# Two feed-forward stacks: a new order of all engines, with the halves of scores and of weighing mostly side by side

## The chip, the cores and the metric
The kernel runs on one core of a Trainium2 chip. The metric is the device time of the whole program in microseconds. Before the change it is 3801.89 us, the median of three runs (3801.88 to 3802.43).

## The reference
The input is a batch of 4 sequences of 512 tokens with 128 features. The residual stream goes through four parts, each on the layer-normed stream: a retention attention, a stack of six layers, an RWKV-like mixer, and the same stack again with the same weights.

```python
x = x + attn_a(layernorm(x)); x = x + stack(layernorm(x))
x = x + attn_b(layernorm(x)); x = x + stack(layernorm(x))

# stack: DEPTH = 6 layers, 16 heads of 64, windows of 32 tokens
for i in range(DEPTH):
    x = attn_layer(shift_tokens(x), Wqkv[i], q_scale[i], k_scale[i], Wo[i]) + x
    x = ffn_layer(shift_tokens(x), ln_g[i], ln_b[i], W1[i], b1[i], W2[i], b2[i]) + x

# attn_layer: q and k are l2-normed per head and rotated; each window of 32 queries
# sees its own and the previous window of keys, masked; softmax; times values; @ Wo
# ffn_layer: layernorm, (xn @ W1 + b1) split in a and gate, a * gelu(gate) @ W2 + b2
```

Everything is float32. The change is in the stack, which runs twice and takes most of the time.

## The kernel before
A stack is cut into 96 **tiles** of 128 tokens (6 layers x 4 sequences x 4 tiles). Four tiles of one sequence in one layer are a **group**; a stack has 24. The group g of a layer needs the residual stream that group g - 4 of the layer before has left. The residual stream of all sequences lies transposed in `xst`, features on partitions.

What a tile goes through, with the engine in brackets: `stage` copies its 128 columns of `xst` to `xs` (GpSimd, L1230); `project` makes six products of 512 columns, k0, q0, k1, q1, v0 and v1, each in one bank of PSUM (TensorE, L584); `rotate` reads a q or k bank twice and multiplies with cosines and sines (VectorE, L1038), `rope` adds these (GpSimd, L1238), `square` reads the same bank (ScalarE, L876), `sum_squares` and `norms` make the inverse lengths (VectorE) with `guess` (ScalarE) between, and `unit` multiplies them in (GpSimd, L1247). `turn` transposes a chunk with four matmuls (L595), `keep` copies it out (ScalarE, L897). `scores` is in two halves of 64 small matmuls on 64x32 parts of the array (L604), into two banks of its own. Then `mask_max`, `off_max`, `exponent`, `sum_probs`, `invert`, `scale_probs`, on VectorE, GpSimd and ScalarE. `turn_probs` transposes the probabilities in two halves, `probs_out` copies them out. `weigh` multiplies with values, in two halves of 64 small matmuls on 64x64 parts (L629). The values come by ten DMAs a tile from `v_nat` to `v_w` (`spread_values`, SyncE, L515) after `values_out`. `heads_out` copies weighed heads out, one half at a time (ScalarE, L936), `project_out` multiplies them with Wo (L647), `mid` adds them to the residual stream (VectorE, L1115).

What a group goes through when its four tiles are done: `center`, `center_square`, `center_out`, `variance`, `inv_std`, `mid_norm`, `gain_bias`; six products `up` (gate and lin, 0 to 2), three `gelu` and three `hidden`, one `down` of three accumulated products, and `finish`, which adds to the stream (VectorE, L1144).

All products but scores and weighing share four PSUM banks, `work`. Which item writes which bank is a table, `BANK`, with an entry for each of the four slots. Both halves of weighing write the same 256 columns of `bank_o`, so the second half of a tile has to wait until the first is copied out, and stands in the next slot.

The order is written out by hand for each engine, in a function `slot(N, T, G, at, of)`. A stack is 96 + 12 **slots**; slot N has T = N mod 4. `at(3)` is tile N - 3, `of(2)` is the group two before this slot's. `run_slots` (L482) unrolls 16 slots, then a loop of two rounds with 32 slots, then 28. On TensorE a wait stands ahead of most items: the bank that it writes must have been read. Such a wait reads `wait(pe, "squared_k0", N - 2)`. In the loop, `apart` puts a count-up of a semaphore between waits and matmuls of scores and weighing.

The order of TensorE before, in slot 1, without its waits:

```
q1(3) gate1 v1(5) weigh1(7) T.q0(4) T.k0(4) P1(6) T.q1(4) k0(2) q0(2) scores0(4) P0(6)
out(7) weigh0(6) T.k1(4) k1(2) v0(4) scores1(4) lin2
```

Here `k0` is a projection, `T.k0` a turn, `P0` a turn of probabilities, `out` is `project_out`; the number in brackets is how many slots the tile is behind. The other three slots have the same tile items in nearly the same order; lin 0 and gate 2 are in slot 0, lin 1 in slot 2, `center` in slot 2, `variance`, `down` and gate 0 in slot 3.

## Time and profile before

| | |
|---|---|
| median of 3 runs | 3801.89 us |
| profiled execution, its span | 3803.9 us |
| TensorE busy | 3594.4 us (94%), 61680 matmuls |
| VectorE busy | 3264.6 us (86%) |
| GpSimd busy | 2752.8 us (72%) |
| ScalarE busy | 2374.7 us (62%) |
| `project`, L592 | 1148.0 us busy, 2304 matmuls, 604 ns each |
| `weigh`, L641 | 437.0 us busy, 24576 matmuls, 221 ns each |
| `scores`, L615 | 330.4 us busy, 24576 matmuls, 224 ns each |
| `square`, L883 | 443.3 us busy, 768 instructions, 594 ns each |
| `stage`, L1236 | 4 in a group, 1.2 us busy, 293 ns each |

A matmul on float32 is two instructions in the profile. Matmuls are pipelined: their durations overlap, so the cost of a group of them is seen from start to start, not from a mean. The profiled execution lasts as long as its span; nothing lies around it. The first stack runs from about 106 to 1736 us, the second from 2171 to 3799.

### The profile page before, as it was taken

What the parts mean: (1) busy time and instruction counts of PE and PEld (TensorE: products, weight loads), DVE (VectorE), ACT (ScalarE), POOL (GpSimd) and SP (SyncE); (2) the same over time, 40 slices, a digit from 0 to 9 for tenths busy, and PEclk for the clock granted to TensorE, in tenths of its full rate; (3) what the DMA queues carried; (4) which work ended last, traced back from release to release, by engine and by line L of the source; (5) the groups of instructions that cost most, each with busy time, mean ns of one, the idle gap of its engine ahead of it and who ended that gap; (6) DMA issues with size and microseconds to landing.
All of it is one profiled execution on the core that took longest, in us unless ns stands there. A gap on an engine that the chain in (4) does not pass through costs nothing. (4 is left out here: it accounts for less than half of the span.)

```text
span 3803.9 us, 157044 instructions
## 1 busy us (share of the span) xinstructions
PE 3594.4 (94%) x61680; PEld 2336.5 (61%) x61680; DVE 3264.6 (86%) x11515; ACT 2374.7 (62%) x4331; POOL 2752.8 (72%) x2632
## 2 busy tenths in 40 slices
PE   6799999999999999997699689999999999999998
PEld 4466666666666666662466456666666666666665
DVE  6898888888888889865799798889898888889885
ACT  2567667666766767663422257667676766767665
POOL 1788888878888888852144288888887888888883
PEclk9899999999999999998799699999999999999999
DMA  1232323323322332220000132233233232332222
GB/s 46 77 85 71 81 73 78 87 67 74 85 73 69 85 75 66 66 65 16 0 1 6 29 81 72 74 87 78 71 80 76 71 81 74 83 78 68 66 69 57
DMA packets 170286, 250.95 MB, mean 66 GB/s; under 512 B 36544, under 2 KB 67264, under 8 KB 169408
## 3 DMA queue, kind: packets, MB, share of 16 engines
q1 hardware_dynamic: 169536, 240.72, 25.4%
q8 instruction: 499, 8.18, 0.9%
q14 instruction: 251, 2.06, 0.2%
HBM read 38.21 MB, written 1.05 MB: 10 GB/s over the span
## 5 line engine op out<-in xcount | busy, mean ns | idle before, releaser
L592 PE MATMUL stack_work<-stack_w_qkv,stack_xs 128*128 128x512 f32 x2304 | 1148.0, 604 | 34.4 <-ACT stack_sq L883 17.8
L1244 POOL TENSOR_TENSOR stack_roped<-stack_rot_c,stack_rot_s 128x512 f32<-128x512 f32 x768 | 984.6, 1304 | 148.5 <-DVE stack_rot_s L1052 148.2
L1254 POOL TENSOR_TENSOR stack_roped<-stack_roped,stack_rnorm 128x512 f32<-128x512 f32 x768 | 794.6, 1045 | 188.7 <-DVE stack_rnorm L1084 188.7
L883 ACT ACTIVATE stack_sq<-stack_work 128x512 f32<-128x512 f32 x768 | 443.3, 594 | 485.6 <-DVE stack_rot_s L1052 485.1
L1050 DVE TENSOR_TENSOR stack_rot_c<-stack_work,rot_tables 128x512 f32<-128x512 f32 x768 | 526.8, 686 | 130.4 <-PE stack_work L592 112.9
L592 PEld LDWEIGHTS stack_work<-stack_w_qkv,stack_xs 128*128 128x128 f32 x2304 | 400.5, 191 | 384.4 <-issue 323.9
L1270 POOL TENSOR_TENSOR stack_s_m<-stack_s_m,stack_inv 128x512 f32<-128x512 f32 x384 | 400.8, 1044 | 276.4 <-DVE stack_inv L1113 276.1
L1052 DVE TENSOR_TENSOR stack_rot_s<-stack_work,rot_tables 128x512 f32<-128x512 f32 x768 | 521.6, 679 | 0.0
L1061 DVE TENSOR_REDUCE stack_ssq<-stack_sq 128x8 f32<-128x512 f32 x768 | 496.7, 667 | 6.0 <-issue 4.4
L641 PEld LDWEIGHTS stack_bank_o<-stack_p_t,stack_v_w 64*64 64x64 f32 x24576 | 394.5, 135 | 171.9 <-issue 147.4
L600 PE MATMUL stack_work<-ident,stack_roped 128*128 128x128 f32 x3072 | 452.2, 280 | 8.3 <-issue 5.8
L1095 DVE CUSTOM_DVE_ANT_0 stack_s_m<-stack_bank_s,band 128x64 f32<-128x64 f32 x3072 | 449.4, 217 | 7.4 <-PE stack_bank_s L615 7.4
L615 PEld LDWEIGHTS stack_bank_s<-stack_k_t,stack_q_t 64*32 64x32 f32 x24576 | 268.3, 105 | 289.1 <-issue 287.4
L641 PE MATMUL stack_bank_o<-stack_p_t,stack_v_w 64*64 64x32 f32 x24576 | 437.0, 221 | 1.4 <-issue 1.4
L1262 POOL TENSOR_TENSOR stack_s_m<-stack_s_m,stack_smax 128x512 f32<-128x512 f32 x384 | 401.2, 1045 | 2.9 <-DVE stack_smax L1095 2.7
L600 PEld LDWEIGHTS stack_work<-ident,stack_roped 128*128 128x128 f32 x3072 | 338.2, 141 | 77.7 <-issue 53.3
L655 PE MATMUL stack_work<-stack_o_t,stack_w_o 128*128 128x128 f32 x3072 | 374.6, 275 | 1.7 <-DVE stack_hid L1141 1.7
L655 PEld LDWEIGHTS stack_work<-stack_o_t,stack_w_o 128*128 128x128 f32 x3072 | 358.1, 192 | 3.3 <-DVE stack_hid L1141 3.3
L676 PE MATMUL stack_work<-stack_x_c,stack_w 128*128 128x512 f32 (+1 forms) x576 | 309.7, 621 | 27.4 <-ACT stack_hid L983 21.7
L615 PE MATMUL stack_bank_s<-stack_k_t,stack_q_t 64*32 64x64 f32 x24576 | 330.4, 224 | 0.0
L909 ACT COPY stack_q_t<-stack_work 128x512 f32<-128x512 f32 x384 | 230.5, 600 | 112.2 <-PE stack_work L600 101.3
L933 ACT COPY stack_p_t<-stack_work 128x512 f32<-128x512 f32 x384 | 228.9, 596 | 56.1 <-PE stack_work L626 55.7
(257 smaller groups left out, 5269.0 us busy)
## 6 DMA issues: line engine op xcount, KB each, us to landing
stack_v_w<-stack_v_nat SPq DMA_DIRECT2D x1152, 128.0 KB
stack_v_w<-stack_v_nat SPq DMA_DIRECT2D x768, 64.0 KB
stack_w_qkv<-table_ffn_qkv SPq DMA_DIRECT2D x192, 96.0 KB, 2.3
stack_w_o<-table_ffn_wo SPq DMA_DIRECT2D x12, 512.0 KB, 4.2
stack_w<-table_ffn_w SPq DMA_DIRECT2D x12, 384.0 KB, 3.3
stack_w<-table_ffn_w SPq DMA_DIRECT2D x12, 192.0 KB, 3.1
x_outer<-L_attn_a_X SPq DMA_DIRECT2D x4, 256.0 KB, 6.9
ret_xpos<-table_xpos SPq DMA_DIRECT2D x1, 1024.0 KB, 6.2
```

The lines of the kernel that those rows point to most:

```text
L592: pe.matmul(bank[:, :], xs[:, T, :], w_qkv[:, g.half, col:col + 512], start=True, stop=True).then_inc(done["proj_" + c], 1)
L600: last = pe.transpose(bank[:, P * n:P * (n + 1)], roped[:, CHUNKS.index(c), T % 2, P * n:P * (n + 1)], ident[:, :])
L615: last = pe.matmul(bank_s[j][WINDOW * n:WINDOW * (n + 1), 64 * hp:64 * hp + 64], q_t[rows, T % 2, hp, WINDOW * n:WINDOW * (n + 1)], k_t[ro ...
L641: last = pe.matmul(bank_o[HD * odd:HD * (odd + 1), gp, at:at + WINDOW], v_w[64 * gp:64 * gp + 64, T % 2, n, 2 * m + j, :], p_t[64 * gp:64 ...
L655: last = pe.matmul(bank[:, 0:P], w_o[:, g.half, n, :], o_t[:, T % 2, n, :], start=n == 0, stop=n == PAIRS - 1)
L883: act.activation(sq[:, i % 2, :], work[(BANK["p_" + c][T] + g.row) % 4][:, :], ACT.Square).then_inc(done["squared_" + c], 1)
L1050: dve.tensor_tensor(rot_c[:, i % 2, :].rearrange("p (h d) -> p h d", h=8), src.rearrange("p (h d) -> p h d", h=8), cosine, ALU.mult)
L1052: dve.tensor_tensor(rot_s[:, i % 2, :].rearrange("p (h f d) -> p h f d", h=8, f=2), src.rearrange("p (h f d) -> p h f d", h=8, f=2)[:, :, ...
L1061: dve.tensor_reduce(ssq[:, T % 2, i, :], sq[:, i % 2, :].rearrange("p (h d) -> p h d", h=8), AX.X, ALU.add).then_inc(done["summed_" + c], 1)
L1095: last = dve.tensor_tensor_reduce(s_m[:, T % 2, j, hp, :], bank_s[j][:, 64 * hp:64 * hp + 64], mask[:, first:first + 2 * WINDOW], 1.0, LOW ...
L1244: pool.tensor_tensor(roped[:, i, T % 2, :], rot_c[:, i % 2, :], rot_s[:, i % 2, :], ALU.add).then_inc(done["roped_" + c], 1)
L1254: pool.tensor_tensor(r, r, rnorm[:, T % 2, i, :].unsqueeze(2).broadcast_to([P, 8, HD]), ALU.mult).then_inc(done["united_" + c], 1)
```

## The change
All six bodies and tables of the order are replaced; the helpers change where they must.

```diff
 # TensorE: reads the residual stream itself
-    pe.matmul(bank[:, :], xs[:, T, :], w_qkv[:, g.half, col:col + 512], start=True, stop=True
+    pe.matmul(work[(BANK["p_" + c][T] + g.row) % 4][:, :], xst[:, g.row, P * T:P * (T + 1)],
+              w_qkv[:, g.half, col:col + 512], start=True, stop=True).then_inc(done["proj_" + c], 1)
 # before the first projection of a tile
-    wait(pe, "staged", t)
+    if c == FIRST_IN and T == 0:
+        wait_x(pe, g.number - BATCH)
...
 # weigh: the halves have columns of their own
-    m, at = 2 * half + odd, P * half + WINDOW * n
+    m, at = 2 * half + odd, P * (2 * j + half) + WINDOW * n
...
 # ScalarE: one copy a tile
-            def heads_out(t, T, g, j):
+            def heads_out(t, T, g):
-                wait(act, f"weighed{j}", t)
+                wait(act, "weighed1", t)
                 wait(act, "pe_wo", t - 2)
-                act.copy(o_t[:, T % 2, 4 * j:4 * j + 4, :].rearrange("p (g h) n -> p g h n", g=2),
-                         bank_o[:, :, 0:2 * P].rearrange("p g (h n) -> p g h n", h=2)
-                         ).then_inc(done[f"ot_set{j}"], 1)
+                act.copy(o_t[:, T % 2, :, :].rearrange("p (j g h) n -> p j g h n", j=2, g=2),
+                         bank_o[:, :, :].rearrange("p g (j h n) -> p j g h n", j=2, h=2)).then_inc(done["ot_set"], 1)
...
 # TensorE, slot 0, the beginning
+                    wait_group(pe, "hid0", G - 3)
+                    project(*at(0), "k0")
+                    wait(pe, "v_out0", N - 3)
+                    turn(*at(2), "q0")
+                    wait(pe, "pt_set0", N - 5)
+                    project(*at(3), "v1")
+                    wait(pe, "ot_set", N - 6)
+                    weigh(*at(5), 0)
+                    wait(pe, "pt_set1", N - 5)
+                    turn(*at(2), "k0")
+                    wait(pe, "squared_k0", N - 0)
+                    up(of(3), "gate", 1)
...
 # GpSimd
-                stage(*at(0))
```

The new order of TensorE, in the notation above:

```
slot 0: k0(0) T.q0(2) v1(3) weigh0(5) T.k0(2) gate1 q0(0) P0(4) weigh1(5) gate2 T.k1(2) out(6)
        T.q1(2) q1(0) lin2 k1(0) scores0(2) scores1(2) T.k1(1) T.k0(1) v0(2) out(5) P1(4) v1(2) T.q0(1)
slot 1: k0(0) T.q1(2) weigh0(5) weigh1(5) lin1 q0(0) P0(4) center k1(0) scores0(2) scores1(2)
        variance P1(4) down v1(2) q1(0) weigh0(4) weigh1(4) T.k0(1) T.q0(1) T.k1(1)
slot 2: k0(0) v0(3) q0(0) scores0(2) T.q1(2) P1(4) q1(0) scores1(2) P0(4) gate0 k1(0)
        weigh0(4) weigh1(4) T.k0(1) v1(2) v0(2)
slot 3: k0(0) out(7) T.q1(2) q0(0) T.q0(2) k1(0) out(6) T.k1(2) q1(0) scores0(2) scores1(2)
        lin0 v0(2) P0(4) P1(4)
```

The orders of ScalarE, VectorE and GpSimd are now also written out for each slot. ScalarE in slot 0, where two gelus of a group stand:

```
square k0(0), values_out 1(3), guess(1), keep k0(2), gelu 1, probs_out 0(4), square q0(0), heads_out(5), gelu 2,
table load, keep k1(2), keep q1(2), exponent 1(3), square q1(0), square k1(0), exponent 0(3), keep k1(1), ...
```

GpSimd has four `rope` and four `unit` in every slot, and beside them three `off_max` and two `scale_probs` in slot 0, two and three in slot 1 (one of the three for the tile four behind), three and none in slot 2, none and three in slot 3. `log_var` and `inv_std` are one function before and two after. The turns back to natural layout at a stack's end stand together in slot 96 + 9.

## Rows read from the trace of the kernel before
**Rows 1.** The page: the span, and a DMA issue with its microseconds to landing.
```profile
span 3803.9 us, 157044 instructions
...
stack_w_qkv<-table_ffn_qkv SPq DMA_DIRECT2D x192, 96.0 KB, 2.3
```
**Rows 2.** Busy us by stretch: TensorE, weight loads, VectorE, ScalarE, GpSimd; granted clock; DMA.
```profile
105.90:228.00 122.10, 105.42 (x1868) 63.65 (x1868) 112.51 (x395) 66.60 (x132) 101.25 (x99) 0.94 0.27 68
...
824.40:895.30 70.90, 66.99 (x1255) 44.07 (x1256) 57.55 (x222) 45.62 (x84) 53.77 (x52) 0.98 0.28 70
1024.05:1089.85 65.80, 65.34 (x1256) 43.14 (x1255) 58.71 (x222) 45.83 (x84) 53.76 (x53) 1.00 0.30 73
```
**Rows 3.** Timeline of VectorE at two neighbouring `finish`: start, us, instruction, idle before.
```profile
1024.05 1.52 DVE L1153 SCALAR_TENSOR_TENSOR stack_xst<-stack_work,stack_vec,stack_mshift 64x512 f32<-64x512 f32 x2 [2.52 <-PE stack_work L685]
...
1089.85 1.52 DVE L1153 SCALAR_TENSOR_TENSOR stack_xst<-stack_work,stack_vec,stack_mshift 64x512 f32<-64x512 f32 x2 [2.52 <-PE stack_work L685]
```
**Rows 4.** Timeline of TensorE's matmuls, from 1042 to 1056 us.
```profile
1042.15 1.95 PE L655 MATMUL stack_work<-stack_o_t,stack_w_o 128*128 128x128 f32 x16
1044.04 1.14 PE L641 MATMUL stack_bank_o<-stack_p_t,stack_v_w 64*64 64x32 f32 x64
1045.10 0.66 PE L600 MATMUL stack_work<-ident,stack_roped 128*128 128x128 f32 x4
1045.59 1.02 PE L592 MATMUL stack_work<-stack_w_qkv,stack_xs 128*128 128x512 f32 x2
1046.45 1.02 PE L676 MATMUL stack_work<-stack_x_c,stack_w 128*85 128x512 f32 x2
1047.31 1.02 PE L592 MATMUL stack_work<-stack_w_qkv,stack_xs 128*128 128x512 f32 x2
1048.26 0.86 PE L615 MATMUL stack_bank_s<-stack_k_t,stack_q_t 64*32 64x64 f32 x64
1049.05 1.12 PE L676 MATMUL stack_work<-stack_x_c,stack_w 128*128 128x512 f32 x2
1050.01 1.02 PE L592 MATMUL stack_work<-stack_w_qkv,stack_xs 128*128 128x512 f32 x2
1051.49 1.12 PE L676 MATMUL stack_work<-stack_x_c,stack_w 128*128 128x512 f32 x2 [0.46 <-ACT stack_hid L983]
...
1053.41 1.14 PE L641 MATMUL stack_bank_o<-stack_p_t,stack_v_w 64*64 64x32 f32 x64
1054.47 1.09 PE L600 MATMUL stack_work<-ident,stack_roped 128*128 128x128 f32 x8
1055.40 0.60 PE L626 MATMUL stack_work<-ident,stack_s_m 128*128 128x128 f32 x4
```
**Rows 5.** Timeline of the weight loads of one half of scores and one of weighing.
```profile
1048.26 0.70 PEld L615 LDWEIGHTS stack_bank_s<-stack_k_t,stack_q_t 64*32 64x32 f32 x64 [0.76 <-issue]
...
1053.41 1.02 PEld L641 LDWEIGHTS stack_bank_o<-stack_p_t,stack_v_w 64*64 64x64 f32 x64 [0.76 <-issue]
```
**Rows 6.** Timeline of ScalarE at the gelu that TensorE waits for.
```profile
1049.46 1.28 ACT L983 ACT_TABLE_LOAD   x1
1050.76 0.68 ACT L983 ACTIVATE stack_hid<-stack_work,stack_vec 85x512 f32<-85x512 f32 x1
```
**Rows 7.** Instructions by line from 1024.1 to 1089.9: count, busy us, mean ns, idle before.
```profile
L941 ACT COPY stack_o_t<-stack_bank_o 128x512 f32<-128x512 f32 x8 | 4.7, 593 | 0.8 <-PE stack_bank_o L641 0.8
...
L1244 POOL TENSOR_TENSOR stack_roped<-stack_rot_c,stack_rot_s 128x512 f32<-128x512 f32 x16 | 20.6, 1308 | 2.8 <-DVE stack_rot_s L1052 2.8
L1254 POOL TENSOR_TENSOR stack_roped<-stack_roped,stack_rnorm 128x512 f32<-128x512 f32 x17 | 17.6, 1044 | 3.9 <-DVE stack_rnorm L1084 3.9
...
L1270 POOL TENSOR_TENSOR stack_s_m<-stack_s_m,stack_inv 128x512 f32<-128x512 f32 x8 | 8.4, 1044 | 5.3 <-DVE stack_inv L1113 5.3
...
L1050 DVE TENSOR_TENSOR stack_rot_c<-stack_work,rot_tables 128x512 f32<-128x512 f32 x16 | 11.0, 687 | 2.3 <-PE stack_work L592 2.0
```
**Rows 8.** Timeline of SyncE's queue: three of a tile's ten value DMAs.
```profile
1056.16 1.87 SPq L531 DMA_DIRECT2D stack_v_w<-stack_v_nat  x3
```

More of the change, by code:

```diff
@@ L661, in center, with variance @@
                 wait(pe, "mid_set", 4 * g.number + 3)
-                pe.matmul(bank[:, :], center_m[:, :], mshift[:, g.pair, 0:SEQ], start=True, stop=True
+                pe.matmul(work[(BANK["ct"] + g.row) % 4][:, :], center_m[:, :], mshift[:, g.pair, 0:SEQ], start=True, stop=True
                           ).then_inc(done["pe_center"], 1)
-            def variance(g, bank):
+            def variance(g):
                 if not live_group(g):
@@ L668, in variance, with up @@
                 wait_group(pe, "center_sq", g)
-                pe.matmul(bank[:, :], mean_m[:, :], c_sq[:, :], start=True, stop=True).then_inc(done["pe_var"], 1)
-            def up(g, kind, k, bank):
+                pe.matmul(work[(BANK["va"] + g.row) % 4][:, :], mean_m[:, :], c_sq[:, :], start=True, stop=True
+                          ).then_inc(done["pe_var"], 1)
+            def up(g, kind, k):
                 if not live_group(g):
@@ new lines, in slot @@
+                    wait(pe, "kept_q0", N - 2)
+                    project(*at(0), "q0")
+                    wait(pe, "v_out1", N - 3)
+                    turn_probs(*at(4), 0)
+                    weigh(*at(5), 1)
+                    wait(pe, "kept_k0", N - 2)
+                    up(of(3), "gate", 2)
+                    wait_group(pe, "gelu1", G - 3)
+                    turn(*at(2), "k1")
+                    wait(pe, "squared_q0", N - 0)
+                    project_out(*at(6))
+                    wait(pe, "pt_set0", N - 4)
@@ new lines, in slot @@
+                    turn(*at(2), "q1")
+                    wait_group(pe, "gelu2", G - 3)
+                    project(*at(0), "q1")
+                    wait(pe, "kept_k1", N - 2)
+                    up(of(3), "lin", 2)
+                    wait(pe, "mid_set", N - 6)
+                    project(*at(0), "k1")
+                    wait(pe, "masked0", N - 3)
+                    wait(pe, "masked1", N - 3)
+                    scores(*at(2), 0)
+                    scores(*at(2), 1)
+                    wait(pe, "kept_q1", N - 2)
@@ new lines, in slot @@
+                    turn(*at(1), "k1")
+                    wait(pe, "squared_q1", N - 0)
+                    turn(*at(1), "k0")
+                    wait_group(pe, "hid2", G - 3)
+                    project(*at(2), "v0")
+                    wait(pe, "squared_k1", N - 0)
+                    project_out(*at(5))
+                    wait(pe, "kept_k1", N - 1)
+                    turn_probs(*at(4), 1)
+                    wait(pe, "kept_k0", N - 1)
+                    project(*at(2), "v1")
+                    wait(pe, "v_out0", N - 2)
@@ L1229, in _ @@
         def _(pool):
-            def stage(t, T, g):
-                if not live(t):
-                    return
-                wait_x(pool, g.number - BATCH)
-                wait(pool, "proj_" + LAST_IN, t - 4)
-                apart(pool, t)
-                pool.tensor_copy(xs[:, T, :], xst[:, g.row, P * T:P * (T + 1)]).then_inc(done["staged"], 1)
             def rope(t, T, g, c):
```

652 lines of the change are left out of this document (374 added, 278 removed).

## The prediction
> **What bounds the kernel now.** I read the page's busy shares first, then busy time by stretch. In one group of four tiles, 1024.05 to 1089.85, TensorE is busy for 65.34 of 65.80 us, VectorE for 58.71, GpSimd for 53.76, ScalarE for 45.83; the granted clock is 1.00, the 2.4 GHz level [rows 2]. So a stack is set by what TensorE is given to do and in what order, and the other three have 11 to 30% to spare. The group is the beat: `finish` (L1153) comes once a group, at 1024.05 and again at 1089.85 [rows 3]. There are 24 groups in a stack, 48 in all. One group of each stack is longer: 824.4 to 895.3 is 70.9 us with TensorE busy for 66.99; that is the loop's way back, which stays. While a stack fills (105.9 to 228) VectorE is busy for 112.5 of 122.1 us: there VectorE decides more than TensorE [rows 2].
>
> Busy is not the same as useful. In TensorE's timeline the difference of two starts is what an item costs. Two projection matmuls with 512 columns (a **pair**, also `up`, `center`, `variance`; `down` is three) cost 0.86 us (1046.45 to 1047.31). `project_out` costs 1.89 in front of a weighing (1042.15 to 1044.04). Four transposes (a **turn**, `turn_probs` too) take 0.49 behind a weighing (1045.10 to 1045.59) and eight take 0.93 there (1054.47 to 1055.40), so one costs 0.435 and the place behind a weighing about 0.06. A half of scores or of weighing is 64 small matmuls on parts of the array; I call it an **island**. It costs 0.79 for scores (1048.26 to 1049.05) and 1.06 for weighing (1053.41 to 1054.47) [rows 4], more than its matmuls, in three places:
> - in front: the pair before one takes 0.95 instead of 0.86 (1047.31 to 1048.26), +0.09; without it `project_out` is 1.80;
> - at its end: scores are busy for 0.86 with a last matmul of 0.22, so that one starts at 0.64, and the next item 0.15 later; weighing 0.92, then 0.14. Steps inside average 0.64/63 = 0.01 and 0.92/63 = 0.015;
> - behind: 0.06 for a turn, as above, and 0.10 for a pair (1049.05 to 1050.01) [rows 4].
> The weight-load queue shows why: the loads of an island start 0.76 us after the load before them has ended, none under the matmul in front [rows 5].
>
> That adds up. Before, a group is 32 pairs x 0.86 = 27.52, 24 turns x 0.435 = 10.44, 4 `project_out` x 1.80 = 7.20, `down` 2.58: 47.74. Islands 8 x 0.79 + 8 x 1.06 = 14.80, 16 fronts x 0.09 = 1.44, behind them 12 turns x 0.06 + 4 pairs x 0.10 = 1.12. Sum 65.10, against 65.80 measured. The missing 0.70 has its place: the pair at 1050.01 lasts until 1051.49, where `up` gate 1 waits for a gelu; it is the only idle time that TensorE's timeline shows in the group [rows 4]. ScalarE gives that gelu behind a table load of 1.28 [rows 6].
>
> **What the change does to that sum.** The matmuls stay the same in number and shape; the stationary operand is read from the residual stream in place of its copy. What goes are borders. In the new order scores are adjacent in slots 0, 1 and 3 and apart in slot 2; weighing is apart in slot 0, adjacent twice in slot 1 and once in slot 2. So 16 islands become 10: three double and two single ones of each kind. 47.74 stays. Double scores cost 0.64 + 0.01 + 0.79 = 1.44, double weighing 0.92 + 0.015 + 1.06 = 2.00, so the islands are 3 x 1.44 + 3 x 2.00 + 2 x 0.79 + 2 x 1.06 = 14.02; 10 fronts 0.90; behind them stand 6 turns (0.36) and 4 pairs (0.40). Sum **63.42**, 1.68 less.
>
> The unknown in it is the joint. Between two halves stand waits (`kept_k1`, `kept_q1`, or `pt_set1`) and in the loop a count-up. No row shows these in the middle of an island. From below they cost nothing; from above as much as an end, a front and what is behind, 0.15 + 0.09 + 0.06, so that next to nothing of 1.68 is left. Weighing is near the lower end: its 64 weight loads are spread over 1.02 us, so instructions arrive faster than they are used. Scores take theirs in 0.70 [rows 5] and have less cover; I give each of their three joints 0.05. That makes 63.57, 1.53 less.
>
> The Trainium skill says in "TensorEngine Tiling (Array Packing)", Key Properties, that changing the tiling mode drains TensorE, while changing only the tile does not. By that rule the joints are free and the sum is 63.42; the trace agrees as to the borders (0.09 in front, 0.15 at the end), and no run here shows a joint.
>
> **What TensorE waits for in the new order.** Each item writes one of four banks, and the next to write it waits for its reader. I take the TensorE time between the two. A square comes after two VectorE instructions of 0.69 [rows 7] and ends its own 0.59, about 2.1 us in all; a copy of 0.59 ends after about 0.75. The shortest distance to a square is the same before and after: pair 0.95, weighing 1.12, two turns 0.87, = 2.95 (after: from k0 in slot 0 to gate 1). The shortest to a copy is three turns, 1.31, before, and four, 1.73, after. Distances of this size hold today, since the one wait is for a gelu [rows 4]. In slot 0 gate 1 now ends 4.7 us after the slot's start and its gelu is asked for at 8.1; table load and gelu are 1.28 + 0.68 [rows 6], and what ScalarE has before them is done by about 4.4. Gate 2 ends at 8.1 and is asked for at 10.7, behind `heads_out` alone. So the 0.70 may go. Tighter is what follows: the table goes back (1.28), then k1 is copied at about 11.0 and asked for at 11.6. I take 0.3 of waiting a group instead of 0.70, between none and 1.5.
>
> `heads_out` is one copy of 1024 columns instead of two of 512 with 0.59 each [rows 7]: between one and two of these, I take 1.05, on an engine busy for 45.8 of 65.8 us. A weighing may start only behind the copy of the tile before; in slot 1 the two are about 10 us apart, so it is hidden, with 8 us of room. The removed staging is 4 x 0.29 us on GpSimd (table above), where nothing waited for it; TensorE waits for the residual itself, finished some three slots earlier. The value DMAs are ten a tile at 0.62 us of issue [rows 8], and a DMA of that queue lands 2.3 us after its issue [rows 1]: 8.5 us. ScalarE's next value copy waits for them: in slots 1 and 2 they can start at 3.4 and 2.3 us and are asked for at 13.7 and 11.8. Hidden by 1 to 2 us.
>
> VectorE's work per group, 58.7 us, stays: 92% of 63.9. GpSimd's 53.8 less 1.2 is 82%, but unevenly spread: slots 2 and 3 last about 25.1 us on TensorE and give GpSimd 8 ropes x 1.31, 8 units x 1.04 and 6 others x 1.04 = 25.1 [rows 7].
>
> **The sum.** 63.57 + 0.30 = 63.87 a group, 1.93 less than 65.80. It counts in 46 of 48 groups: while a stack fills, VectorE covers one group's worth. 46 x 1.93 = 88.8. Fill and drain I leave as they are (`finish` comes 13 slots after a group's first projection instead of 12), with 8 us each way. The profiled execution is its span, 3803.9 us [rows 1]: 3803.9 - 88.8 = 3715.1. It is 2.0 above the median of the runs, 3801.89, so I forecast **3713 us**.
>
> **Rivals.**
> - **A. The joints cost like borders.** For it: nothing in the trace shows a joint. Against: the loads of an island follow each other without a pause [rows 5]. Then only waiting falls by 0.4: 46 x 0.4 = 18, 3784. Half of it is 46 x 1.24 = 57, 3745.
> - **B. New waits eat a part.** The order of four engines is new, and ScalarE has 0.6 us of room behind the table load. At 1.5 us a group instead of 0.30: 46 x (65.80 - 65.07) = 34, 3768.
> - **C. GpSimd becomes the bound (the other side).** Its place is slots 2 and 3, with 25.1 us of work in 25.1 us. Today it idles for 12.0 of 65.8 us, waiting for VectorE's inverses, norms and rotations (5.3, 3.9 and 2.8) [rows 7]. If it idles there in the same share, 4.6 us, and slots 0 and 1 don't catch up, a group takes 63.57 + 4.6 = 68.2: 46 x 2.4 = 109 more, 3911. From 2.2 us of lost time a group on it is slower than before; at 3 us it is 3837. Against: turns lie one or two slots behind their units, so that slots 0 and 1 can catch up.
> - **D. Fill and drain get longer** by what the groups save: that needs 44 us a stack, a third of the whole fill's 122 us [rows 2]. Nothing speaks for it.
>
> **How the numbers follow.** My case 0.62, with its own range 3690 to 3740. A 0.10, of it 0.03 at no change; B 0.14; C 0.10; D 0.01; better than 3690 (no waiting at all, 48 x 2.38 = 114) 0.03. A measurement of this kernel tells 0.2% (7.6 us) from no change. Faster 0.86, same 0.03, slower 0.11. The range goes down to all of the islands and waits and 8 us of fill (3680), and up to the middle of A and B and some way beyond: 3785.
>
> **What would show it.** Right: two `finish` of neighbouring groups 63.4 to 64.2 us apart; double scores of 1.4 to 1.5 us and double weighing of 2.0 from start to the next item; ten fronts of 0.09; the gelu wait gone or moved; `heads_out` x192 of about 1.05 us. Wrong, by the joint: double scores over 1.6. Wrong, by waits: TensorE rows with idle time behind a square, a copy or a united chunk, and GpSimd busy over 90% in a group.

## The result, and the profile after
The changed kernel takes **3844.76 us** (median of 4 runs, 3843.56 to 3848.38) against 3802.16 (3801.88 to 3806.66) for the kernel before: ratio 1.0107, 95% interval 1.0093 to 1.012. It is 1.1% slower; the forecast was 2.3% faster. The page of the changed kernel:
```profile
span 3843.6 us, 156240 instructions
...
PE 3557.4 (93%) x61680; PEld 2340.8 (61%) x61680; DVE 3250.6 (85%) x11515; ACT 2368.7 (62%) x4135; POOL 2707.1 (70%) x2440
...
L591 PE MATMUL stack_work<-stack_w_qkv,stack_xst 128*128 128x512 f32 x2304 | 1175.4, 607 | 71.4 <-ACT stack_sq L885 43.2
...
L1112 DVE TENSOR_REDUCE stack_ssq<-stack_sq 128x8 f32<-128x512 f32 x768 | 513.9, 669 | 70.1 <-ACT stack_sq L885 69.6
...
L642 PE MATMUL stack_bank_o<-stack_p_t,stack_v_w 64*64 64x32 f32 x24576 | 415.6, 220 | 16.0 <-issue 14.5
...
L615 PE MATMUL stack_bank_s<-stack_k_t,stack_q_t 64*32 64x64 f32 x24576 | 320.8, 225 | 33.9 <-issue 33.9
```
TensorE's busy time fell, as forecast, its idle time rose by more. Idle time grew in two places: behind a square (L885), 43.2 us at the projections against 17.8 before, with 69.6 us of VectorE's that the kernel before does not have; and "issue" in scores and weighing, which was 0.0 and 1.4 us before.

Busy time by stretch (columns as in [rows 2]): the fill of stack 1, the twenty groups behind it, and one group without a stop inside an island, 65.44 us, that answers to the 65.80 of [rows 2]:
```profile
106.70:308.80 202.10, 177.16 (x3269) 112.14 (x3270) 175.70 (x648) 117.05 (x219) 163.27 (x149) 0.94 0.28 70
308.80:1645.00 1336.20, 1294.18 (x25081) 865.26 (x25081) 1166.47 (x4440) 916.14 (x1601) 1055.27 (x960) 1.00 0.30 74
1120.47:1185.91 65.44, 64.24 (x1255) 42.91 (x1254) 58.94 (x223) 44.88 (x80) 51.96 (x48) 1.00 0.31 76
```
Cut at `finish`, stack 1 is: fill (first projection to first `finish`) 202.1 us against 189.1, twenty groups 1336.2 against 1321.5, drain 116.6 against 118.9. Stack 2: 200.0 against 188.8, 1337.7 against 1321.9, 108.5 against 116.1. Groups were 65.8 each; now they run from 65.3 to 70.8 (72.6 and 72.8 at the loop's way back, 70.9 and 71.2 before). The long ones are the first after the fill and after the loop's way back.

TensorE's timeline in the first group of the twenty (columns as in [rows 4]) shows what was right and the first thing that was missed:
```profile
322.37 2.07 PE L642 MATMUL stack_bank_o<-stack_p_t,stack_v_w 64*64 64x32 f32 x128
324.37 0.66 PE L600 MATMUL stack_work<-ident,stack_roped 128*128 128x128 f32 x4
324.86 1.88 PE L591 MATMUL stack_work<-stack_w_qkv,stack_xst 128*128 128x512 f32 x4
327.41 1.12 PE L591 MATMUL stack_work<-stack_w_qkv,stack_xst 128*128 128x512 f32 x2 [0.66 <-ACT stack_sq L885]
...
332.46 1.12 PE L591 MATMUL stack_work<-stack_w_qkv,stack_xst 128*128 128x512 f32 x2 [0.41 <-DVE stack_mshift L1174]
```
Double weighing costs 324.37 - 322.37 = 2.00 us, exactly the sum's number. In double scores the step from the first half's last matmul to the second half's first is 0.017 us (median of 144), less than the longest steps inside every half (0.03 to 0.06): the **joint is free**. By the Trainium skill ("TensorEngine Tiling (Array Packing)", Key Properties) a change of tile alone drains nothing; the runs agree, with 0.017 us across the joint and 2.00 for double weighing.

The whole account of the group without a stop can be read from TensorE's rows:
```profile
1136.38 1.89 PE L591 MATMUL stack_work<-stack_w_qkv,stack_xst 128*128 128x512 f32 x4
1139.05 1.13 PE L591 MATMUL stack_work<-stack_w_qkv,stack_xst 128*128 128x512 f32 x2 [0.78 <-ACT stack_sq L885]
1140.01 1.95 PE L656 MATMUL stack_work<-stack_o_t,stack_w_o 128*128 128x128 f32 x16
...
1143.10 0.60 PE L600 MATMUL stack_work<-ident,stack_roped 128*128 128x128 f32 x4
1144.12 1.12 PE L591 MATMUL stack_work<-stack_w_qkv,stack_xst 128*128 128x512 f32 x2 [0.42 <-DVE stack_mshift L1174]
1145.08 1.95 PE L656 MATMUL stack_work<-stack_o_t,stack_w_o 128*128 128x128 f32 x16
...
1148.25 1.51 PE L615 MATMUL stack_bank_s<-stack_k_t,stack_q_t 64*32 64x64 f32 x128
1149.69 1.12 PE L679 MATMUL stack_work<-stack_x_c,stack_w 128*128 128x512 f32 x2
...
1165.77 1.60 PE L615 MATMUL stack_bank_s<-stack_k_t,stack_q_t 64*32 64x64 f32 x128
1167.30 1.09 PE L600 MATMUL stack_work<-ident,stack_roped 128*128 128x128 f32 x8
...
1180.07 1.73 PE L615 MATMUL stack_bank_s<-stack_k_t,stack_q_t 64*32 64x64 f32 x128
1181.73 1.13 PE L670 MATMUL stack_work<-stack_c_sq,stack_mean_m 128*128 128x512 f32 x2
```
The group lasts 65.44 us, 2.02 more than the 63.42 of the prediction's sum. From start to start, against the sum's costs, the wait for a square takes 1.05 us (0.95, and 0.10 in the pair behind it), the wait for `mid` (L1174) 0.68 (0.58 and 0.10). The three double scores cost 1.44, 1.53 and 1.66 instead of three times 1.44, together 0.31, all of it in their second halves. That makes 2.04.

The wait at 327.41 comes back 66.2 us later, at 393.58, and in 13 of the twenty groups in all. It is for square k1. ScalarE's timeline in the slot with tile 2:
```profile
322.85 0.60 ACT L885 ACTIVATE stack_sq<-stack_work 128x512 f32<-128x512 f32 x1 [1.50 <-DVE stack_rot_s L1103]
323.46 1.28 ACT L991 ACT_TABLE_LOAD   x1
324.76 0.69 ACT L991 ACTIVATE stack_hid<-stack_work,stack_vec 128x512 f32<-128x512 f32 x1
325.46 1.28 ACT L1058 ACT_TABLE_LOAD   x1
326.76 0.60 ACT L885 ACTIVATE stack_sq<-stack_work 128x512 f32<-128x512 f32 x1
```
and VectorE's beside it:
```profile
322.74 0.68 DVE L1101 TENSOR_TENSOR stack_rot_c<-stack_work,rot_tables 128x512 f32<-128x512 f32 x1
323.33 0.67 DVE L1103 TENSOR_TENSOR stack_rot_s<-stack_work,rot_tables 128x512 f32<-128x512 f32 x1
...
327.39 0.69 DVE L1112 TENSOR_REDUCE stack_ssq<-stack_sq 128x8 f32<-128x512 f32 x1 [1.57 <-ACT stack_sq L885]
```
The rotation of k1 ends at 324.0, its square starts at 326.76, behind gelu 0 and two table loads. TensorE and VectorE both wait for it.

The second thing missed stands inside an island. Here 128 matmuls of scores are cut behind the 101st:
```profile
537.59 1.26 PE L615 MATMUL stack_bank_s<-stack_k_t,stack_q_t 64*32 64x64 f32 x101
540.69 0.66 PE L615 MATMUL stack_bank_s<-stack_k_t,stack_q_t 64*32 64x64 f32 x27 [1.84 <-issue]
541.28 2.07 PE L679 MATMUL stack_work<-stack_x_c,stack_w 128*128 128x512 f32 x2
543.15 1.49 PE L591 MATMUL stack_work<-stack_w_qkv,stack_xst 128*128 128x512 f32 x2
```
No wait stands there in the program. The DMA view of 537.5 to 538 (queue, kind, packets, MB, share) has the answer:
```profile
q8 instruction: 1, 0.02, 16.2%
```
That packet carries 16384 bytes and is under way from 537.94 to 539.24. The whole run has 497 of them for TensorE's 61680 matmuls and as many loads: one piece for some 256 instructions. I call such a stop a **pause**, and count every step of over 0.15 us between the starts of two neighbouring matmuls of an island (steps that come from missing records are left out). There are 70 in the changed kernel, 63.6 us in all, 65 of them inside a half, and none before. (Over 0.30 us there are 61, with 62.0 us.) Each ends a median of 1.40 us after the landing of such a piece, 2.6 us after its start, and then the clock can be down too (windows, granted clock third from the end):
```profile
537.00:540.60 3.60, 1.85 (x103) 1.13 (x102) 3.06 (x7) 2.38 (x4) 3.60 (x4) 1.00 0.26 71
540.70:544.10 3.40, 3.40 (x31) 1.68 (x31) 0.70 (x2) 0.56 (x2) 2.43 (x3) 0.50 0.00 0
544.20:548.00 3.80, 3.80 (x46) 2.24 (x44) 3.43 (x7) 2.42 (x5) 1.89 (x2) 1.00 0.02 4
```
For 3.4 us the granted clock is 0.50, the 1.2 GHz level: the pair at 541.28 takes 1.87 us instead of 0.96.

Pauses and waits are not independent. In the last four of the twenty groups a pause of 0.83 to 1.10 us stands in a weighing some 2 us ahead of the place of the square wait; the square wait is gone there, and the groups last 65.6 to 65.7 us, hardly more than the 65.3 to 65.4 without a pause.

### The profile page after: what moved, and what is told of

Read it like the earlier page. It is cut to its first block and busy times, and to the rows that moved or that the text cites. A ratio compares the mean times of both kernels' runs of the same rounds, so it can differ in the third digit from the quotient of the medians.

```text
span 3843.6 us, 156240 instructions
## 1 busy us (share of the span) xinstructions
PE 3557.4 (93%) x61680; PEld 2340.8 (61%) x61680; DVE 3250.6 (85%) x11515; ACT 2368.7 (62%) x4135; POOL 2707.1 (70%) x2440
## 3 DMA queue, kind: packets, MB, share of 16 engines
HBM read 38.21 MB, written 1.05 MB: 10 GB/s over the span
## 5 line engine op out<-in xcount | busy, mean ns | idle before, releaser
L591 PE MATMUL stack_work<-stack_w_qkv,stack_xst 128*128 128x512 f32 x2304 | 1175.4, 607 | 71.4 <-ACT stack_sq L885 43.2
L885 ACT ACTIVATE stack_sq<-stack_work 128x512 f32<-128x512 f32 x768 | 459.0, 598 | 596.1 <-DVE stack_rot_s L1103 590.6
L1353 POOL TENSOR_TENSOR stack_roped<-stack_roped,stack_rnorm 128x512 f32<-128x512 f32 x768 | 791.2, 1043 | 45.8 <-DVE stack_rnorm L1135 45.8
L591 PEld LDWEIGHTS stack_work<-stack_w_qkv,stack_xst 128*128 128x128 f32 x2304 | 390.6, 193 | 382.1 <-issue 257.3
L1112 DVE TENSOR_REDUCE stack_ssq<-stack_sq 128x8 f32<-128x512 f32 x768 | 513.9, 669 | 70.1 <-ACT stack_sq L885 69.6
L1361 POOL TENSOR_TENSOR stack_s_m<-stack_s_m,stack_smax 128x512 f32<-128x512 f32 x384 | 415.0, 1081 | 174.4 <-DVE stack_smax L1146 174.4
L1146 DVE CUSTOM_DVE_ANT_0 stack_s_m<-stack_bank_s,band 128x64 f32<-128x64 f32 x3072 | 464.2, 214 | 6.3 <-PE stack_bank_s L615 4.4
L600 PEld LDWEIGHTS stack_work<-ident,stack_roped 128*128 128x128 f32 x3072 | 353.3, 141 | 167.6 <-issue 113.4
L642 PE MATMUL stack_bank_o<-stack_p_t,stack_v_w 64*64 64x32 f32 x24576 | 415.6, 220 | 16.0 <-issue 14.5
L656 PEld LDWEIGHTS stack_work<-stack_o_t,stack_w_o 128*128 128x128 f32 x3072 | 369.0, 192 | 73.1 <-issue 64.5
L1156 DVE TENSOR_REDUCE stack_psum_p<-stack_s_m 128x8 f32<-128x512 f32 x384 | 255.7, 675 | 16.1 <-ACT stack_s_m L928 14.4
```

Of the source, the lines that this page charges most:

```text
L591: pe.matmul(work[(BANK["p_" + c][T] + g.row) % 4][:, :], xst[:, g.row, P * T:P * (T + 1)], w_qkv[:, g.half, col:col + 512], start=True, st ...
L600: last = pe.transpose(bank[:, P * n:P * (n + 1)], roped[:, CHUNKS.index(c), T % 2, P * n:P * (n + 1)], ident[:, :])
L642: last = pe.matmul(bank_o[HD * odd:HD * (odd + 1), gp, at:at + WINDOW], v_w[64 * gp:64 * gp + 64, T % 2, n, 2 * m + j, :], p_t[64 * gp:64 ...
L656: last = pe.matmul(bank[:, 0:P], w_o[:, g.half, n, :], o_t[:, T % 2, n, :], start=n == 0, stop=n == PAIRS - 1)
L885: act.activation(sq[:, i % 2, :], work[(BANK["p_" + c][T] + g.row) % 4][:, :], ACT.Square).then_inc(done["squared_" + c], 1)
L1112: dve.tensor_reduce(ssq[:, T % 2, i, :], sq[:, i % 2, :].rearrange("p (h d) -> p h d", h=8), AX.X, ALU.add).then_inc(done["summed_" + c], 1)
```

## The experiments
Theories: **N**, TensorE's items cost what the sum says. **R**, the order ties TensorE to the round trip through VectorE and ScalarE. **F**, pauses are late instructions. Each kernel is compared with the kernel before, run beside it.

### One part alone, and parts undone
**b_scores**: the kernel before with the two halves of scores adjacent in every slot. **b_weigh**: the kernel before with the weighing adjacent, in columns of its own, one `heads_out`.
```diff
-                    wait(pe, "masked1", N - 5)
-                    scores(*at(4), 0)
 ...
+                    wait(pe, "masked1", N - 5)
+                    scores(*at(4), 0)
                     scores(*at(4), 1)
 ...  # b_weigh
-                    weigh(*at(7), 1)
+                    weigh(*at(7), 0)
+                    weigh(*at(7), 1)
-                    weigh(*at(6), 0)
```


> The kernel before with one thing changed: in each slot the first half of scores moves down to stand right in front of the second (192 double islands of 128 matmuls). Theory F (TensorE's own instructions arrive late: 16 KB pieces of 256 instructions on the instruction queue, and a double island is 256 instructions in 1.44 us): pauses of 0.2 to 2 us inside some of the double islands, ended by nothing in the profile and each 1.2 to 1.5 us after the landing of such a piece; they eat what the borders give back, 3785 to 3825 us. Rival W (the new order's own waits made the change slow, double islands are fine): no pauses, every double island 1.44 us, 192 x 0.29 = 56 us gained, 3745 us. Rival J (the joint itself costs like a border): double islands of 1.6 to 1.7 us all alike, 3790 to 3802.

> The kernel before with weighing as in the change and nothing else: columns of their own for both halves, both halves adjacent behind each other in the slot of the second, one copy of the heads per tile. Theory F: fewer pauses than with scores, since 128 weighing matmuls take 2.0 us instead of 1.44; 192 x 0.29 = 56 gained less some 20 to 40 for pauses, 3765 to 3785. Rival W: 3746 and no pauses. Rival that heads_out with 1.0 us or its later place is a new wait: TensorE idle behind it, over 3802.

Measured: b_scores 3834.21 us, ratio 1.0079 (1.0062 to 1.0096); b_weigh 3859.94, 1.0151 (1.0134 to 1.0169). Both are slower than the upper ends of theory F's ranges (3825 and 3785), and b_weigh has more pauses than b_scores (20 against 11), not fewer. Double scores cost 1.44, so by the sum a group falls to about 63.9 and 64.0; they last 66.2 and 66.7, with 2.0 and 4.8 us of pauses in twenty groups. b_scores, one group:
```profile
1506.35 1.13 PE L592 MATMUL stack_work<-stack_w_qkv,stack_xs 128*128 128x512 f32 x2 [0.29 <-ACT stack_sq L883]
...
1527.76 1.12 PE L676 MATMUL stack_work<-stack_x_c,stack_w 128*128 128x512 f32 x2 [0.73 <-ACT stack_hid L983]
...
1550.11 0.66 PE L626 MATMUL stack_work<-ident,stack_s_m 128*128 128x128 f32 x4 [0.38 <-DVE stack_hid L1141]
```
Where an island goes, its time no longer covers a square or a gelu. So adjacency alone loses, by new waits. In b_weigh they are behind squares (0.38, 0.26 and 0.25 us of idle time in a group) and a gelu (0.15), none behind `heads_out`, so its last rival had the side right and the reason wrong.

**a_split_s** and **a_split**: the changed kernel with the double scores split by a projection; then the double weighing too.
```diff
-                    project(*at(0), "k1")
                     scores(*at(2), 0)
+                    project(*at(0), "k1")
                     scores(*at(2), 1)
```


> The changed kernel with its three double scores of a group split again: the projection that stood in front of them stands between the halves. Nothing else moves. Theory F: the pauses inside scores (about 37 in two stacks, 47 us) and the clock drops behind them go; 144 borders of 0.29 come back (42 us). So about the same, 3815 to 3845, with the groups after the fill and after the loop's way back now as long as the others. Rival W: only the borders count, 3885 us, and groups as uneven as before.

> The same with the three double weighings of a group split too (one item between the halves). Theory F: no pause inside any island is left, all borders are back: nominal 65.0 us a group plus the waits of the new order, 1.0 to 2.0; 3810 to 3850 us. Rival W: 3844 + 84 = 3928 us. What is left above 65.0 us a group in this kernel is the price of the new order's own waits.

Measured: 3851.31, 1.0116 (1.0098 to 1.0135), and 3868.79, 1.0177 (1.0157 to 1.0196); groups 66.1 and 66.5 at their quietest, pauses 47 (40.7 us) and 36 (28.5 us). a_split is slower than the changed kernel clear of noise; the total of a_split_s can't be told apart from it. The borders come back and cost more than the pauses that go: adjacency pays in this order, yet doesn't pay enough.

Here F as I had put it failed: a_split should have had no pause inside any island, and 32 of its 36 stand in islands of a single half. One:
```profile
941.92 1.12 PE L591 MATMUL stack_work<-stack_w_qkv,stack_xst 128*128 128x512 f32 x2
942.98 0.77 PE L615 MATMUL stack_bank_s<-stack_k_t,stack_q_t 64*32 64x64 f32 x55
944.90 0.32 PE L615 MATMUL stack_bank_s<-stack_k_t,stack_q_t 64*32 64x64 f32 x9 [1.15 <-issue]
```
What counts is how fast 256 instructions are used, whether or not a single item stands between. In the twenty groups TensorE's fastest 256 take 3.52 us in the kernel before (no pause), 2.42 in a_split and 1.28 in the changed kernel.

### Whose round trip is it
Three engines made lighter, one at a time, in the changed kernel. a_dve leaves out half of the sine product, a_act half of the square, a_pool half of the scaling by the norms; **b_dve** is a_dve's edit on the kernel before.
```diff
-                dve.tensor_tensor(rot_s[:, i % 2, :]...   # 512 columns
+                dve.tensor_tensor(rot_s[:, i % 2, 0:256]...
```


> The changed kernel with the sine product of rotate on half of its 512 columns (it leaves out half of the sine products): some 0.27 us less on VectorE 16 times a group, 4.3 us of 58. Theory L (the beat is no longer TensorE's sum but the way round over VectorE: a bank is free only when VectorE, in its own order, has rotated it, and then ScalarE has squared it): the waits of TensorE for squares and mid shrink, settled groups fall from 65.5 to 63.6 to 64.5 us; with 46 groups 3760 to 3800 us. Rival: VectorE is not in the way, only the instruction supply and ScalarE; then within 10 us of 3844.

> The changed kernel with square on half of its 512 columns (it leaves out half of the squares): 0.21 us less on ScalarE 16 times a group, 3.4 us of 45.5. If ScalarE's order (table loads of 1.28 ahead of copies) is what TensorE waits for, settled groups fall by over 1 us and the time below 3800; by theory L only the 0.2 us at the end of each square counts, once or twice a group: 3820 to 3840.

> The changed kernel with unit on half of its 512 columns (it leaves out half of the scaling by inverse lengths): 0.5 us less on GpSimd 16 times a group, 8 us of 52. My forecast's rival C (GpSimd is the bound in slots 2 and 3): below 3800 us. Theory L allows it a part, since VectorE waits for rope before it rotates the next chunk but one: 3810 to 3840. If it has room: 3844.

> The kernel before with VectorE's sine product on half of its columns (it leaves out half of the sine products), which took 69 us from the changed kernel. If the kernel before is bound by TensorE alone, as the prediction has it (65.34 of 65.80 busy, one wait of 0.7 behind gelu), groups stay 65.8 or fall by at most the 0.7, and the whole by 0 to 30 us. If its beat too hangs on the round trip through VectorE, groups fall by 1 us or more and the whole by over 45 us, and the change's loss is then not a new kind of wait.

Measured: a_dve 3775.29, 0.9921 (0.9901 to 0.9941): 69 us below the changed kernel. a_act 3828.8, 1.0069 (1.0052 to 1.0086). a_pool 3823.97, 1.0053 (1.0033 to 1.0073). b_dve 3775.03, 0.9917 (0.9901 to 0.9934): 31.6 below its kernel before, groups 65.2 to 65.4 where the sum of the kernel before says 65.10. So the kernel before has only its 0.7 a group to win, and is bound by TensorE; the changed one wins twice as much by a lighter VectorE, and meets b_dve at the same time. GpSimd, 6.9 us a group lighter (613 instead of 1043 ns, 16 times), gives 21 us: rival C is not the cause.

**a_light**: all three, and half of the cosine product too.

> The changed kernel with half of the columns left out in four steps of the round trip: both rotation products on VectorE, the square on ScalarE, the scaling by the norms on GpSimd. TensorE's work is whole. If TensorE's items cost what the prediction's sum says and all else is waits for the other engines, groups without a pause inside an island come to 63.4 to 63.7 us (settled groups now 65.4), and the whole to 3735 to 3765, the pauses (about 60 us) included. Rival: the items are dearer than the sum (the joint, the borders): then quiet groups stay over 64.2 even so. Theory F expects the pauses to be as many as in the changed kernel or more (50 to 80 us), since a TensorE that waits less draws its instructions faster.

Measured: 3754.99, 0.9875 (0.9855 to 0.9895). The quietest groups are 63.7 and 63.9, against 63.42 in the sum. All waits of TensorE over 0.15 us from 300 to 460 us are pauses:
```profile
354.08 0.32 PE L615 MATMUL stack_bank_s<-stack_k_t,stack_q_t 64*32 64x64 f32 x9 [0.84 <-issue]
419.50 0.38 PE L615 MATMUL stack_bank_s<-stack_k_t,stack_q_t 64*32 64x64 f32 x18 [1.09 <-issue]
451.70 0.41 PE L615 MATMUL stack_bank_s<-stack_k_t,stack_q_t 64*32 64x64 f32 x18 [0.16 <-issue]
```
N holds (double scores have medians of 1.44, 1.52 and 1.54 here, by their place, which is some 0.2 of the 0.3 that is left), R is the larger part, F stays (83 pauses). The fill falls from 202.1 and 200.0 to 186.6 in both stacks, so its 11 to 13 us are waits for the other engines as well; with VectorE alone lighter it is 194.1 and 192.8 (a_dve) against 185.4 and 183.4 (b_dve).

**a_fix**: the longer of the two waits that the timelines name. ScalarE's square k1 ahead of gelu 0 in the slot with tile 2.
```diff
+                    square(*at(0), "k1")
                     gelu(of(2), 0)
                     if live_group(G - 2) and not is_slot(G - 2, GROUPS - 1):
                         act.preload_act_table_set(TABLE)
-                    square(*at(0), "k1")
```


> The changed kernel with two ScalarE steps of the slot with tile 2 exchanged: the square of k1 ahead of gelu 0 and its two table loads. Nothing else. In the changed kernel the square of k1 stands 3.25 us behind the end of the rotation (table load 1.28, gelu 0.69, table load 1.28), and TensorE's projection in that bank then idles 1.07 us with 0.58 us more behind it, VectorE's sum of squares 1.57 us. Theory W (the new order put the path of the banks behind gelu's table loads): settled groups fall from 65.4 to 64.0 to 64.6 us, 30 to 55 us of the whole. Rival R (the round trip through VectorE's fixed order holds the beat, and the wait only moves to the next square): groups stay over 65.1, the whole within 15 us of the changed kernel. Rival F (what TensorE's pauses inside islands cost is separate): the 63 pauses inside halves stay, 55 to 65 us, under either.

Measured: 3841.58, 1.0089 (1.0071 to 1.0106); 3 us below the changed kernel, which is within noise. Groups at least 65.1, against 65.3. The wait for the square is gone and this one is there instead, every 65.7 us:
```profile
322.43 1.98 PE L591 MATMUL stack_work<-stack_w_qkv,stack_xst 128*128 128x512 f32 x4 [0.83 <-ACT stack_hid L991]
...
388.15 1.99 PE L591 MATMUL stack_work<-stack_w_qkv,stack_xst 128*128 128x512 f32 x4 [0.82 <-ACT stack_hid L991]
```
The next bank belongs to gelu 0, and is free 0.6 us later than before. That is what R expects: the exchange moves the wait. 3.85 us of ScalarE (two loads, gelu, square) have to fit between two users of neighbouring banks. Whether another exchange would heal it wasn't tried.

### The pauses
**a_shift**: 128 instructions more at TensorE's start, nothing else.
```diff
+            for _ in range(128):
+                pe.sem_inc(padded, 1)
             pe.wait_ge(w_in, 32)
             turn_in(0)
```


> The changed kernel with 128 more TensorE instructions (increments of a semaphore that nobody waits for) ahead of all its work, where TensorE waits for its first weights until 8 us anyway. No step of the stacks is touched; only the place of each TensorE instruction in the stream of 16384-byte pieces (256 instructions) moves by half a piece. Theory F (pauses inside an island are TensorE's instructions that come too late, one piece at a time): the pauses that now stand at matmuls 119, 110, 101, 93 of double islands in the first groups stand 64 matmuls earlier or later (55, 46, 37, 29), or in other islands; long groups are others than now; the whole moves by up to 20 us either way. Rival H (they are waits of another kind, bound to the work's own order, such as a PSUM bank's reader): same groups, same positions, same time within 5 us.

Measured: 3837.3, 1.0078 (1.0062 to 1.0095). 42 pauses instead of 70, not 64 matmuls earlier in the same islands but late in other ones (mostly at matmuls 113 to 124, before 91 to 127), and other groups are the long ones. The prologue cost 12 us (first projection at 119.1, was 106.7), the stacks are 15.2 and 7.6 us shorter. Only the place in the stream moved, so F holds and H falls. The total is barely clear of the changed kernel's (1.0093 to 1.012); the places of the pauses decide it, not the time.

**a_twice**: every half of the scores computed twice in a row.
```diff
-                for hp in range(4 * part, 4 * part + 4):
+                for hp in 2 * list(range(4 * part, 4 * part + 4)):
```


> The changed kernel with every half of the scores computed twice in a row into the same places: a double island is then 256 matmuls with 256 weight loads, 512 instructions, and the output is the same. Each group gets 4 x 1.44 = 5.8 us of TensorE work, and the other engines that much slack, so that waits for them vanish: without a limit of supply a group is 63.4 + 5.8 = 69.2 to 69.6 us. Theory F (instructions come in pieces of 16384 bytes, 256 instructions, no closer than about 3 us): an island of 512 instructions in 2.88 us runs into the limit whatever its phase; pauses inside halves in nearly every one of the 184 islands, 0.5 to 3 us each, groups 71 to 80 us, and pieces land 2.9 to 3.5 us apart at their closest. Rival H (pauses come from the work's order): pauses as few as now, under 0.4 us per island.

Measured: 4590.68, 1.2048 (1.202 to 1.2076); groups 77.9 to 85.9, 88.1 at the loop's way back. The page and TensorE's timeline:
```profile
q8 instruction: 689, 11.29, 1.1%
```
```profile
1039.32 2.13 PE L615 MATMUL stack_bank_s<-stack_k_t,stack_q_t 64*32 64x64 f32 x186
1042.94 0.95 PE L615 MATMUL stack_bank_s<-stack_k_t,stack_q_t 64*32 64x64 f32 x70 [1.48 <-issue]
```
192 pieces more for 2 x 24576 more instructions, which is 256 each. 270 pauses with 423 us; they end 1.39 us after a landing and 2.5 after its start (medians). The work added is 46 x 5.8 = 265 us, the time added 746. Groups are longer than F's 71 to 80; pauses are most of it, and the mean granted clock over the twenty groups is 0.95 instead of 1.00.

**a_unroll** and **b_unroll**: the loop written out, in the changed kernel and in the one before.
```diff
-            with eng.Fori(0, 2) as pair:
+            for pair in range(2):
```


> The changed kernel with the loop of 2 x 32 slots written out as 64 slots. The way back (5 us a stack) goes: 3834 us. Theory F, pauses belong to places in the instruction stream and come again in each round at the same place: with the stream written out they stand at other places in the two rounds, so that the pattern of long groups (the first four of each round) is gone; their sum may be larger or smaller. Rival (pauses belong to the schedule's state behind a disturbance): without the way back the second series of long groups is gone altogether, 3820 us.

> The kernel before with the loop over its middle slots written out (two rounds of 32 slots each, twice), no branch left. The loop's border costs it 70.9 and 71.2 against 65.8 us in a group of each stack: without it 8 to 12 us less, unless the longer program's instructions come late. Theory F says that its single islands (64 instructions and others between them) need pieces no faster than they come: no pauses, groups 65.8 all through. Were the changed kernel's irregular groups under unrolling due to the unrolling itself and not to the double islands, they would be seen here as well, and the gain gone.

Measured: a_unroll 3825.06, 1.0052 (1.0036 to 1.0069); twenty groups take 1342.9 us in stack 1, with 29.8 of pauses, and 1314.0 in stack 2, with 14.5. b_unroll 3791.06, 0.9963 (0.9949 to 0.9977), every group of the middle 65.8 or 65.9, one pause of 0.2 us in the whole run. Irregular groups come with islands close together, not with unrolling.

### A version better than both
**b_nostage**: the change's last part alone. **b_swap**: b_unroll with v1's projection ahead of gate 1 in slot 1. **b_short**: b_unroll and b_nostage together.
```diff
 # b_nostage
-                stage(*at(0))
-    pe.matmul(bank[:, :], xs[:, T, :], w_qkv...
+    pe.matmul(bank[:, :], xst[:, g.row, P * T:P * (T + 1)], w_qkv...
 # b_swap
-                    wait_group(pe, "gelu2", G - 3)
-                    up(of(3), "gate", 1, work[(0 + row) % 4])
                     wait(pe, "v_out0", N - 5)
                     project(*at(5), "v1", work[(1 + row) % 4])
+                    wait_group(pe, "gelu2", G - 3)
+                    up(of(3), "gate", 1, work[(0 + row) % 4])
```


> The kernel before without the staged copies of the inputs alone (GpSimd's copy of each tile's input is gone, and the projections read the stack's input itself), as the change does it; nothing else is touched. TensorE's order is the same, GpSimd gets 192 copies less. Prediction's view: worth nothing where TensorE sets the beat, groups 65.8, the whole within 5 us of the kernel before. Rival: the projections now wait for the input's own write at a group's border and make the fill of each stack longer (it is 202 against 189 us in the changed kernel): then the first group ends over 5 us later per stack, and the whole is 8 to 25 us longer.

> The kernel before with its loop written out (3791 by itself) and with one exchange on TensorE: in the slot with tile 1 the projection of v1 ahead of the gate chunk 1, which waits 0.6 to 0.7 us for gelu 2 in each group. If that is the last wait of TensorE's beat, groups fall from 65.8 to 65.2 or 65.3 and the whole to 3765 to 3778, the time that half of the sine product bought. Rival: the gate chunk 0.86 us later makes gelu 1 and the squares behind it on ScalarE late, and the wait comes back in the same slot: groups 65.6 to 66.2, 3785 to 3810.

> The kernel before with its loop written out and without the staged copies of the inputs: the two edits that bought 15.5 and 14.5 us alone. The first takes 5 us at a group's border in each stack, the second 0.2 to 0.3 us of each of some 40 groups. They act in different places, so they should add up: groups of 65.5 or 65.6 all through, none of 70, 3774 to 3782, ratio 0.992 to 0.9945. Rival: without the loop's border the copies' absence makes a projection wait for the input's write at some border: 3785 or more. Theory F expects no pause inside a single island (at most one or two).

Measured: b_nostage 3792.68, 0.9968 (0.9956 to 0.9979), groups 65.6, fill 188.1 and 188.9: the part costs nothing in the fill and brings 14 us, where I had put nothing. b_swap 3812.96, 1.0018 (1.0008 to 1.0028), so 22 us worse than b_unroll, with groups of 66.3; this is slower than both ranges expected. In place of the gelu wait stands
```profile
1516.80 1.13 PE L592 MATMUL stack_work<-stack_w_qkv,stack_xs 128*128 128x512 f32 x2 [0.92 <-ACT stack_v_nat L917]
```
b_short **3778.64**, 0.993 (0.9916 to 0.9943): the two edits add up (0.9963 x 0.9968 = 0.9931), and it is the fastest version that computes everything, 24 us under the kernel before and 66 under the changed one.

## Why the prediction was wrong
Twenty middle groups of stack 1, in us. "Sum" is 20 times the prediction's sum of items plus 5 for the loop's way back; "pauses" are the stops inside islands; "rest" is what is left, TensorE's waits with the overlap that they destroy, the slower second halves of double scores, and what stretches at a granted clock of 0.50 lose (10.2 us of such stretches in the changed kernel, 3.4 in the kernel before and in a_shift, none in a_dve and a_light; half of them is lost at most):

```
            twenty groups   sum     pauses  rest   rest per group
before          1321.5      1307.0    0.0   14.5   0.7
b_dve           1313.6      1307.0    0.0    6.6   0.3
changed         1336.2      1273.4   24.1   38.7   1.9
a_shift         1323.9      1273.4   12.3   38.2   1.9
a_fix           1335.6      1273.4   26.7   35.5   1.8
a_dve           1308.5      1273.4   23.5   11.6   0.6
a_light         1300.5      1273.4   20.2    6.9   0.3
```

- **The sum of items** (65.10, then 63.42) was right but for scores. a_light's quietest groups are 63.7, and its rest is 0.3.
- **The joint** is free: nothing instead of my 0.05, and rival A falls. But two of the three double scores of a group cost 1.53 and 1.66 instead of 1.44, by slower second halves: 0.31 a group, where three joints of 0.05 had been allowed for.
- **The step that failed is "What TensorE waits for in the new order"**: I took 0.3 us a group; the rest measures 1.9, of it 1.73 in two waits in the group without a pause (1.05 behind a square, 0.68 behind `mid`). Rival B had 1.5. I compared distances on TensorE (2.95 us before and after) with the sum of a reader's durations (2.1 us), as if the reader took each bank at once. It takes it at its place in its own fixed order. I had followed gelu 1 and 2 in slot 0 and never gelu 0 in slot 2, whose two table loads stand between rotation and square k1. That row is not the whole: a_fix removed it and another wait took its place, while a lighter VectorE removed 1.3 us a group. That VectorE would be busy for 92% of the beat should have been a term, not a remark.
- **A term was missing**: pauses, 1.2 to 1.35 us a group. From [rows 5] I wrote that in weighing "instructions arrive faster than they are used". That was the state of a stream already there; no row of before shows what happens when 256 instructions are used in 1.44 or 2.00 us; there the fastest 256 take 3.52. In a_shift the term is about one to one over twenty groups: 11.8 us of pauses less, 12.3 us less time. Group by group it isn't, since a pause can take the place of a wait.
- **Fill**: taken as unchanged, with 8 us each way; it was +13.0 and +11.2, together 24 of the 45 us by which the stacks grew. a_light puts it to waits for VectorE and the others, as in the middle groups. Rival D, "nothing speaks for it", named the place but asked for 44 us a stack, and took 122 us for the whole fill; up to the first `finish` it is 189.
- **GpSimd (rival C)** did not bind: busy for 52.0 of 65.4 us. The kernel did become slower, as C has it, but by another way.
- `heads_out` was right: 1011 ns x192, forecast 1.05.

The account of both stacks: fill +24.2, middle +30.5, drain -9.9; the parts outside them -5.

What stays open: why the second halves of double scores are slower even without a pause; why the instruction piece is asked for so late; and which step of VectorE's or ScalarE's order would have to move for both waits to go.

## What to carry to other kernels
Costs saved on the busiest engine count only if each of its buffers is still free in time: walk through the readers' own orders, table loads included, and treat a reader that is as busy as VectorE here (90% of the group) as a second bound. Before packing small matmuls close together, count instructions: a stretch that uses a whole 16384-byte piece (here 256) in less than the 2.6 us from a piece's start to its use can pause. Whether it does depends on where the pieces end: b_scores has 192 double islands and 11 pauses. Try the dull parts of a large change alone: here the loop's end and a staging copy were worth 24 us together, while the whole change cost 42.

## What the runs showed of the hardware
- TensorE's instructions come by DMA in pieces of 16384 bytes, 256 instructions, asked for while it runs: start of the piece to resumption 2.6 us (median of 70), landing to resumption 1.40 (1.39 in a_twice, with 270; of the changed kernel's 61 pauses over 0.30 us the middle half lies between 1.31 and 1.45). No row links this to other DMA traffic: the DMA share is 0.26 around the pause shown, against 0.30 over the twenty groups.
- Islands needn't touch for it: a_split, with an item between the halves of the double islands, has 36 pauses where its fastest 256 instructions take 2.42 us; the kernel before, at 3.52, has none.
- Whether an island pauses depends on where its instructions lie in the stream: 128 count-ups of a semaphore at the start left 42 of 70 pauses.
- A pause of 1.84 us was followed by 3.4 us at a granted clock of 0.50, so it cost more than itself.
- Two halves of scores or of weighing side by side have no border between them: from the 64th matmul's start to the 65th's it is 0.017 us in scores and 0.039 in weighing (medians of 144).
- Idle time in a row understates a wait: the kernel before shows 0.46 for what costs 0.70 [rows 4], the changed one 0.78 and 0.42 for 1.05 and 0.68.
